# The Mamba state scan, cut into units of 32 channels times four states, with some of its B products on TensorE

## What is computed

```python
xdbl = jnp.einsum('ble,fe->blf', xc, xproj)           # xc: 512 channels, after conv and silu
dt = jax.nn.softplus(jnp.einsum('blr,er->ble', xdbl[..., :R], dtw) + dtb)
Bm, Cm = xdbl[..., R:R + NS], xdbl[..., R + NS:]      # NS = 16 states
def step(h, inp):
    dt_t, B_t, C_t, x_t = inp
    dA = jnp.exp(dt_t[..., None] * A)                 # A = -exp(Alog), one number per channel and state
    h = dA * h + (dt_t * x_t)[..., None] * B_t[:, None, :]
    y = jnp.einsum('ben,bn->be', h, C_t)
    return (h, y)
y = ssm_scan(dt, Bm, Cm, xc, A) + xc * Dp
y = y * jax.nn.silu(z)
```

## Times and profile before

| | |
|---|---|
| median of 3 runs | 3189.39 us (3189.24 to 3197.11) |
| the profiled execution | 3177.29 us |
| its span, first to last instruction | 3175.4 us |
| mean granted TensorE clock | 0.911 of full speed |
| layer 0 mixers, first to last scan | from 103.3 to 1051.3 us |
| layer 1 mixers | four chunks, to about 2808 us |

### The profile page before, as it was taken

How to read it: one execution, slowest core, us unless ns; L and a number is a source line. 1 busy time by engine, 2 the same in 40 slices (tenths; PEclk the granted TensorE clock), 3 DMA queues, 4 the chain that set the end, 5 groups by cost and what they waited for, 6 DMA issues and landing times. The chain is left out here.

```text
span 3175.4 us, 27412 instructions
## 1 busy us (share of the span) xinstructions
PE 2544.1 (80%) x8312; PEld 1195.9 (38%) x8312; DVE 1973.9 (62%) x2687; ACT 1386.0 (44%) x2120; POOL 1538.4 (48%) x1350
## 2 busy tenths in 40 slices
PE   5889989889978687678888459998488988768866
PEld 1333323333322254323333258886132332225422
DVE  1799999999999444666663400001349999953423
ACT  4566566566554333215555212221346555432243
POOL 2699999999998301300000320001449999940100
PEclk8999999999999889869999679998689999988887
DMA  1220220230220000253210434453222022000000
GB/s 65 108 107 24 106 108 22 92 114 8 99 107 0 20 1 0 89 66 41 41 21 2 148 119 173 173 192 114 65 107 84 24 106 106 2 20 0 0 8 27
DMA packets 69153, 215.25 MB, mean 68 GB/s; under 512 B 13692, under 2 KB 38536, under 8 KB 49944
## 3 DMA queue, kind: packets, MB, share of 16 engines
q1 hardware_dynamic: 62632, 181.11, 17.4%
q10 hardware_dynamic: 3312, 24.12, 2.3%
q0 software_dynamic: 3072, 8.39, 0.8%
HBM read 187.97 MB, written 25.43 MB: 67 GB/s over the span
## 5 line engine op out<-in xcount | busy, mean ns | idle before, releaser
L775 POOL TENSOR_TENSOR s_dbu<-s_dx,s_bc 128x512 f32<-128x512 f32 x768 | 964.6, 1281 | 47.2 <-DVE s_psum L509 43.4
L436 PE MATMUL s_psum<-s_hc,ident 128*128 128x512 f32 x1536 | 834.0, 633 | 174.1 <-DVE s_hc L529 163.0
L664 ACT ACTIVATE s_psum<-s_dt,s_a_neg 128x512 f32<-128x512 f32 x768 | 521.6, 688 | 586.1 <-DVE s_hc L529 585.1
L436 PEld LDWEIGHTS s_psum<-s_hc,ident 128*128 128x128 f32 x1536 | 260.3, 193 | 686.1 <-DVE s_hc L529 488.8
L529 DVE TENSOR_TENSOR s_hc<-s_psum,s_bc 128x512 f32<-128x512 f32 x624 | 421.8, 676 | 0.5 <-issue 0.5
L509 DVE TENSOR_TENSOR_SCAN s_psum<-s_psum,s_state,s_dbu 128x512 f32<-128x512 f32 x312 | 396.4, 1282 | 18.6 <-ACT s_psum L664 12.7
L509 DVE TENSOR_TENSOR_SCAN s_psum<-s_psum,s_dbu 128x512 f32<-128x512 f32 x312 | 381.4, 1223 | 22.1 <-ACT s_psum L664 14.2
L1467 ACT ACTIVATE s_probs<-s_banks 128x512 f32<-128x512 f32 (+3 forms) x384 | 169.7, 492 | 206.2 <-PE s_banks L1290 163.5
L163 POOL TENSOR_TENSOR s_pair<-s_res 128x512 f32<-128x512 f32 x8 | 10.0, 1267 | 416.0 <-issue 403.3
L1837 ACT ACTIVATE s_hidden<-s_banks,s_w 128x256 f32<-128x256 f32 x184 | 77.3, 471 | 302.3 <-PE s_banks L1660 302.3
L1858 POOL DMA_INDIRECT s_rows_in<-moe_out_rows,s_place x32 | 30.7, 958 | 358.4 <-DMA moe_out_rows<-s_ys 349.0
(11 more groups left out here) (260 smaller groups left out, 3638.1 us busy)
## 6 DMA issues: line engine op xcount, KB each, us to landing
s_bc<-fwd_rows SPq DMA_DIRECT2D x64, 1024.0 KB, 4.6
s_bc<-m_rows SPq DMA_DIRECT2D x32, 1024.0 KB, 4.7
s_w<-in_moe_w SPq DMA_DIRECT2D x23, 1028.0 KB, 7.2
s_w<-in_moe_w ACTq DMA_DIRECT2D x23, 1024.0 KB, 5.5
qk_parts<-s_parts SPq DMA_DIRECT2D x48, 128.0 KB, 1.9
s_stack_q<-qk_parts SPq DMA_DIRECT2D x48, 128.0 KB, 4.9
s_stack_k<-qk_parts SPq DMA_DIRECT2D x48, 128.0 KB, 8.2
moe_in_rows<-s_zero SPq DMA_DIRECT2D x1, 5888.0 KB, 18.9
```

Source lines behind the costliest of these rows:

```text
L436: pe.matmul(psum[:, SCANS + block_no % 2, :], consts["ident"][:], hc[:, unit % PRODUCTS, :], start=(n == 0), stop=(n == NS - 1)).then_inc( ...
L664: act.activation(psum[:, unit % SCANS, :], dt[:, g % 2, i // NS, :], ACT.Exp, scale=a_neg[CHUNKS[g][0]][:, i:i + 1]).then_inc(decay_ready, 1)
L775: pool.tensor_tensor(dbu[:, unit % TERMS, :], dx[:, g % 2, i // NS, :], bc[:, 2 * n, :], ALU.mult)\
```

## The change

A unit is now 32 channels times four states. Unit i has its block q = i // 16, a group n of four states and a strip j of 32 channels (`split`); partition r * 32 + e of its tile is state 4n + r of channel 32j + e.

- dt and dx have to stand four times, once for each r. Each block of both is stored to DRAM and read back by four DMAs of 32 partitions into `dt_rep` and `dx_rep` (two buffers each). B and C are spread by DMAs to 32 partitions; a tile of `b_rows` or `c_rows` then serves all strips and blocks.
- The sum over states: `total` multiplies with `fold` (four 32 x 32 identities on top of each other) and writes the 32 partitions of its strip. Four totals are now issued together, at every fourth unit.
- In 24 of 64 units (`TURNED`) the term dx * B is made by PE, in `turn_term`: 16 matmuls of transposed dx (stationary, 32 columns) with diagonal matrices of B (moving, 128 columns), into the unit's PSUM bank; ACT's decay goes to a `dbu` buffer there. PE does it three units ahead of the scan's, or four (`TURN_AT`). PE also transposes B and dx once a chunk (20 transposes), and ACT stores these and makes 32 diagonals of 128 x 128 (`make_diag`).
- `LENT` has 28 units in place of 12. Their scans write straight into `hc`, and POOL multiplies in place, `LAG` = 4 units later; in even chunks it first copies the last column to `state` and waits for that copy.
- `TERMS` is 4, `PRODUCTS` is 8. The remaining steps have new unit numbers; three of four gates are done within their own chunk.

The core of the diff (the second product, dx's store and spread and C's spread are written like their neighbours):

```diff
@@ -216,19 +216,51 @@
                 act.activation(rstd[:, c, :], rstd[:, c, :], ACT.Exp, scale=-0.5).then_inc(rstd_ready, 1)
 
 
+STRIP = 32
+STRIPS = P // STRIP
+GROUPS = NS // STRIPS
 UNITS = EB * NS
-SCANS, TERMS, PRODUCTS = 4, 3, 4
-LENT = [i < 3 * NS and i % 4 == 2 for i in range(UNITS)]
+SCANS, TERMS, PRODUCTS, LAG = 4, 4, 8, 4
+DIAG = (1, 3)
+LENT = [i in LENT_AT for LENT_AT in ((1, 3, 5, 7, 9, 11, 12, 13), (1, 2, 4, 5, 7, 9, 11, 12, 13), (5, 7, 12, 13),
+                                     (1, 3, 5, 7, 9, 12, 13)) for i in range(NS)]
+TURNED = [i % NS in (5, 7, 12, 13, 14, 15) for i in range(UNITS)]
+TURN_AT = {}
+for i in range(UNITS):
+    if TURNED[i]:
+        TURN_AT.setdefault(i - 4 if i % STRIPS == STRIPS - 1 else i - 3, []).append(i)
+MADE = [n for n in range(GROUPS) if not all(TURNED[n * STRIPS:(n + 1) * STRIPS])]
+KEEPS = sum(not (LENT[i] and LENT[i - 1]) for i in range(1, UNITS, 2))
...
+def split(i):
+
+    return i // NS, i // STRIPS % GROUPS, i % STRIPS
...
-        dt = s.sb("dt", [P, 2, EB, CH])
+        dt = s.sb("dt", [P, EB, CH])
-        bc = s.sb("bc", [P, 2 * NS, CH])
+        b_rows = s.sb("b_rows", [P, len(MADE), CH])
+        c_rows = s.sb("c_rows", [P, GROUPS, CH])
+        dt_rep = s.sb("dt_rep", [P, 2, STRIPS, CH])
+        dx_rep = s.sb("dx_rep", [P, 2, STRIPS, CH])
+        diag = s.sb("diag", [P, len(DIAG), STRIPS, CH // P, P])
+        b_cols = s.sb("b_cols", [P, CH // P, NS])
-        hs = s.sb("hs", [P, CH])
+        dt_d = core.nc.dram_tensor(f"{first}_steps", (2, EI, CH), F32, kind="Internal").ap()
+        dx_d = core.nc.dram_tensor(f"{first}_inputs", (2, EI, CH), F32, kind="Internal").ap()
...
-        for kind, count in (("x", EB), ("conv", EB), ("rows", 1), ("dt", EB)):
+        for kind, count in (("x", EB), ("conv", EB), ("rows", 1), ("dt", EB), ("cols", 1), ("turn", CH // P)):
...
-            def spread(g, n):
-                sp.dma_start(bc[:, 2 * n:2 * n + 4, :], rows_d[g % 2, 2 * n:2 * n + 4, :].partition_broadcast(P))\
-                  .then_inc(row_loaded[n // 2], 16)
+            def spread_b(g, n):
+
+                if g:
+                    sp.wait_ge(dbu_ready, made(g * UNITS - NS + (n + 1) * STRIPS))
+                for r in range(STRIPS):
+                    sp.dma_start(b_rows[r * STRIP:(r + 1) * STRIP, MADE.index(n), :],
+                                 rows_d[g % 2, 2 * (n * STRIPS + r), :].partition_broadcast(STRIP)).then_inc(b_loaded[MADE.index(n)], 16)
...
+            def store_dt(g, e):
+                sp.wait_ge(dt_ready, EB * g + e + 1)
+                sp.dma_start(dt_d[g % 2, e * P:(e + 1) * P, :], dt[:, e, :]).then_inc(dt_stored[e], 16)
+
...
+            def spread_dt(g, q):
+                block_no = EB * g + q
+                if block_no >= 2:
+                    sp.wait_ge(decay_ready, (block_no - 1) * NS)
+                sp.wait_ge(dt_stored[q], 16 * (g + 1))
+                for r in range(STRIPS):
+                    sp.dma_start(dt_rep[r * STRIP:(r + 1) * STRIP, q % 2, :, :],
+                                 dt_d[g % 2, q * P:(q + 1) * P, :].rearrange("(j e) t -> e j t", j=STRIPS))\
+                      .then_inc(dt_spread[q % 2], 16)
...
             store_rows(0)
-            for n in range(0, NS, 2):
-                spread(0, n)
+            for n in MADE:
+                spread_b(0, n)
+            for n in range(GROUPS - 1):
+                spread_c(0, n)
+            for q in range(2):
+                store_dt(0, q)
+                store_dx(0, q)
...
+            def turn_term(g, i):
+
+                unit = g * UNITS + i
+                q, n, j = split(i)
+                at = DIAG.index(n)
+                if unit >= SCANS and LENT[(unit - SCANS) % UNITS]:
+                    pe.wait_ge(scanned, unit - SCANS + 1)
+                elif unit >= SCANS:
+                    pe.wait_ge(product_ready, own(unit - SCANS + 1))
+                for w in (tile["turn", g, CH // P - 2], tile["turn", g, CH // P - 1]):
+                    pe.wait_ge(work_free[w % 2], w // 2 + 1)
+                pe.wait_ge(diag_ready, NS * (len(DIAG) * g + at + 1))
+                for b in range(CH // P):
+                    for r in range(STRIPS):
+                        mm = pe.matmul(psum[r * STRIP:(r + 1) * STRIP, unit % SCANS, b * P:(b + 1) * P],
+                                       turned_dx(g)[:, q, b, j * STRIP:(j + 1) * STRIP], diag[:, at, r, b, :],
+                                       start=True, stop=True)
+                mm.then_inc(term_turned, 1)
...
-                pe.matmul(psum[:, SCANS + block_no % 2, :], consts["ident"][:], hc[:, unit % PRODUCTS, :],
-                          start=(n == 0), stop=(n == NS - 1)).then_inc(product_used, 1)
+                pe.matmul(psum[j * STRIP:(j + 1) * STRIP, SCANS + block_no % 2, :], fold[:], hc[:, unit % PRODUCTS, :],
+                          start=(n == 0), stop=(n == GROUPS - 1)).then_inc(product_used, 1)
...
                 for i in range(UNITS):
-                    total(g, i)
-                    if g + 1 < NC and i < 16:
-                        conv(g + 1, i // TAPS, i % TAPS)
-                    if g and 16 <= i < 24:
-                        out(g - 1, (i - 16) // EB, i % EB)
-                    if g + 1 < NC and 24 <= i < 28:
-                        rows(g + 1, i - 24)
-                    if g + 1 < NC and i in (30, 31, 34, 35):
-                        steps_of(g + 1, (30, 31, 34, 35).index(i))
-                    if g and post is not None and 36 <= i < 38:
-                        var(g - 1, i - 36)
-                    if i in (38, 39) or 42 <= i < 48:
-                        in_z(g, (38, 42, 44, 46).index(i - i % KD), i % KD)
-                    if g + 2 < NC and 50 <= i < 58:
-                        in_x(g + 2, (i - 50) // KD, i % KD)
+                    for ahead in TURN_AT.get(i, ()):
+                        turn_term(g, ahead)
+                    if i % STRIPS == STRIPS - 1:
+                        for j in range(STRIPS):
+                            total(g, i - STRIPS + 1 + j)
+                    if g + 1 < NC and i < 8:
+                        conv(g + 1, i // 2, i % 2 * 2)
...
-                dve.wait_ge(dbu_ready, unit + 1)
-                h = psum[:, unit % SCANS, :]
-                if LENT[i] and lent(unit):
-                    dve.wait_ge(product_lent, lent(unit))
-                dve.tensor_tensor_scan(hs[:] if LENT[i] else h, h, dbu[:, unit % TERMS, :], begin, ALU.mult, ALU.add)\
-                   .then_inc(scanned, 1)
+                left, right = psum[:, unit % SCANS, :], dbu[:, unit % TERMS, :]
+                if TURNED[i]:
+                    dve.wait_ge(term_turned, turned(unit + 1))
+                    left, right = right, left
+                else:
+                    dve.wait_ge(dbu_ready, made(unit + 1))
+                if LENT[i] and unit >= PRODUCTS:
+                    dve.wait_ge(product_used, unit - PRODUCTS + 1)
+                h = hc[:, unit % PRODUCTS, :] if LENT[i] else psum[:, unit % SCANS, :]
+                dve.tensor_tensor_scan(h, left, right, begin, ALU.mult, ALU.add).then_inc(scanned, 1)
...
+                q, n, j = split(i)
+                to = psum[:, unit % SCANS, :]
                 if i % NS == 0:
-                    act.wait_ge(dt_ready, unit // NS + 1)
-                if unit >= SCANS and LENT[(unit - SCANS) % UNITS]:
+                    act.wait_ge(dt_spread[q % 2], 16 * STRIPS * (unit // NS // 2 + 1))
+                if TURNED[i]:
+                    to = dbu[:, unit % TERMS, :]
+                    if unit >= TERMS:
+                        act.wait_ge(scanned, unit - TERMS + 1)
+                elif unit >= SCANS and LENT[(unit - SCANS) % UNITS]:
                     act.wait_ge(scanned, unit - SCANS + 1)
                 elif unit >= SCANS:
                     act.wait_ge(product_ready, own(unit - SCANS + 1))
-                act.activation(psum[:, unit % SCANS, :], dt[:, g % 2, i // NS, :], ACT.Exp,
-                               scale=a_neg[CHUNKS[g][0]][:, i:i + 1]).then_inc(decay_ready, 1)
-
-            act.wait_ge(small_loaded, 32 * len(runs))
+                act.activation(to, dt_rep[:, q % 2, j, :], ACT.Exp, scale=a_neg[CHUNKS[g][0]][:, i:i + 1]).then_inc(decay_ready, 1)
...
+            def make_diag(g, at, k):
+
+                n, r, b = DIAG[at], k // (CH // P), k % (CH // P)
+                if g and k == 0:
+                    act.wait_ge(term_turned, turned(g * UNITS - NS + (n + 1) * STRIPS))
+                w = tile["cols", g, 0]
+                act.wait_ge(work_free[w % 2], w // 2 + 1)
+                act.activation(diag[:, at, r, b, :], consts["ident"][:], ACT.Copy,
+                               scale=b_cols[:, b, n * STRIPS + r:n * STRIPS + r + 1]).then_inc(diag_ready, 1)
...
-                    pool.wait_ge(dx_ready, unit // NS + 1)
+                q, n, j = split(i)
+                if i % NS == 0:
```

(35 more changed lines are left out.)

262 lines of the change are left out of this document (194 added, 68 removed).

## The result

| | before | after |
|---|---|---|
| median of the runs, us | 3189.3 (3185.4 to 3197.1, 4 runs) | 3318.3 (3315.5 to 3320.8, 4 runs) |
| profiled execution's span, us | 3175.4 | 3319.0 |
| mean granted TensorE clock, share of 2.4 GHz | 0.911 | 0.875 |
| ratio to before | 1 | 1.041 (1.038 to 1.043) |

The change makes the kernel 4.1% slower. The forecast was 3132 us and its range ended at 3210: wrong in sign and outside the range.

A forecast was written before the change was run, and what follows sets the result against it. DVE and POOL were taken to bound the kernel together. Twelve chunks at 5.6 us less gave -67, the two starts +10, so -57: profiled execution 3120, median 3132 us, range 3075 to 3210.

The forecast's parts named there:

- The start: Start of each call: stores and spreads of dt and dx delay the first scan from 103.3 to 108.3, 5 us.
- what is queued behind it: PE's waits at fours: the next turned terms, which DVE's scan needs, stand behind; covered by the extra microsecond of stalls.
- The bound: Mixer chunks: POOL's 109.3 us in even, DVE's 103.0 in odd, mean 106.2 against 112.8; with stalls 5.6 less a chunk.
- PE: 94 us of about 112, 84%: PE's work in a whole chunk: totals, turned units, other matmuls and transposes sum to 94 us, within the chunk's time.
- the 105: Sign of being wrong: PE above 105 us in a chunk.
- the microsecond of stalls: Each chunk: 1.0 us added to 4.5 of stalls, for more evenly loaded engines and PE's queue behind waits.
- Rival 3: Ahead of units 12 to 15 PE brings turned terms too late: 9.6 us a chunk longer, 3235 us; chance 0.08.
- If that is POOL's, it comes four units late: PE waits at each four of totals for the last product; counted within 1.0 us of extra stalls a chunk.
- I leave the clock as it is: TensorE clock in the mixers: taken as unchanged, 0.99 and 1.00 in the windows with PE at 90%.
- Rival 2: PE's fours of totals overlap only in part: 2.15 us each, 3206, chance 0.06; not at all: near 3450, chance 0.02.
- rival 4: ACT's longer stream eats the gain: new stalls of 5 us a chunk, 3189 within 10; chance 0.05.
- Rival 1: Deeper TERMS and PRODUCTS buffers also remove stalls, leaving 1.5 us a chunk: 9.6 less a chunk, 3084; chance 0.20.

The follow-up runs named there:

- e4_lent: Changed kernel with POOL's products moved off the last unit of each four (units 3, 7, 11 to 2, 6, 10): ratio 1.024 to the kernel before.
- e3_diag_once: Changed kernel making the 32 diagonals in the first chunk of each call only (output not the reference's): ratio 1.041 to the kernel before.
- e14_three: Changed kernel with all stores before spreads, POOL's products off each four's last unit, and three of four convolution matmuls omitted after a call's first chunk: 3184.2 us, ratio 0.998.
- e1_start: Changed kernel with the stores of all four blocks of dt and dx issued ahead of the first spread: ratio 1.029 to the kernel before.

## Why the prediction was wrong, point by point

The forecast put the profiled execution at 3120 us, and it took 3321. Of these 201 us, 46 are the two starts, 138 the twelve chunks and 17 the time outside the calls, for which the forecast had nothing.

- **The start, forecast +5 us a call, measured +28.** The failed step is "four spreads of dt and four of dx take 3.8 us to issue, so to 103.4, the last lands 3.5 us later". The issue was right (99.71 to 103.36), and the first spread landed 3.3 us after its issue, near the 3.5 taken. But the eight landed 1.2 us apart and not 0.47, so the last came at 111.3 in place of 106.9; this path would have cost 9 us by itself (111.4 + 1.2 - 103.3). The trace before had shown this: the eight spreads of the earlier trace rows, 1 MB each and issued in 3.8 us, landed 2.5 us apart, the first after 4.5 us and the eighth after 18.6, of which the median in the earlier trace rows tells nothing. The other 19 us are a path that had no term: ACT's copy of the turned dx, a new instruction ahead of the first decay, waits for all four blocks, and SP issues the stores of two of them behind block 1's spreads. The prediction had asked of a wait "what is queued behind it" only for PE.
- **The bound, forecast 5.6 us a chunk less; measured 8.1 more in ten chunks, 5.3 less in two.** The loads of DVE and POOL were right. The failed step is "PE: 94 us of about 112, 84%", a chunk's sum held against a chunk's time. PE's in-order stream had 30.8 us of work for the first quarter, in which DVE takes 26. The sum was low besides: PE is busy 102.0 us in chunk 1, where little of the clock is lost, and 107 to 109 in four of layer 0's eight chunks, over the 105 that the prediction named as a sign of being wrong.
- **The last chunks' 5.3 us are no success of the forecast.** They are odd chunks, and for an odd one its loads say 112.3 to 103.0, 9.3 less, or 8.3 with the microsecond of stalls. DVE's busy time did fall so (112.4 to 104.0 and 110.3 to 100.8), but its idle time rose from 2.5 and 2.0 us to 5.5 and 6.2. That this comes near the mean of 5.6 is chance.
- **Rival 3** named the place (units 12 to 15) and the in-order queue. Its "up to three other matmuls between them" is right for the terms among themselves; what it left out is ahead of them, eleven matmuls of 512 columns between the four of units 0 to 3 and unit 12's term. Its price was 2.4 us at each of four places, 9.6 a chunk; measured are 62.4 us in eight chunks, 7.8 each, but unevenly: 5.2 to 5.9 us in the first quarter, 0 to 3.3 in the others. Its 3235 fell short because it kept the forecast's start, stalls and clock, and its chance of 0.08 was far too low. The sentence that DVE's idle time on PE would be over 20 us in layer 0 if it held proved the right mark: 62 us.
- **"If that is POOL's, it comes four units late"** was written down as part of 1.0 us of stalls a chunk. It measured 52 us in twelve chunks (e4_lent), 4.3 each, a part of it through the clock: the term of the sum that was mis-sized most in the chunks.
- **"I leave the clock as it is"** failed. The mean granted clock of the ten chunks' second quarters is 0.86, in the kernel before 1.00, and a quarter that falls costs about 5 us. The earlier trace rows could not show this, for they are taken with a PE that had a total to do at every unit.
- **Rival 2, refuted.** Eight records of four totals, each total with its own wait and increment, take 524.11 - 523.13 = 0.98 us. Taken singly, the four totals' first records start from 523.135 to 523.155, and only then their second ones, which carry the increments, from 523.564 to 523.584; one record after the other takes 0.43. The Trainium skill, "TensorE: Matmul & The Clock Gate", Part 3, has matmuls start and end in strict program order. This trace does not agree for the records of float32 matmuls: a total's second record stands ahead of the next total's first in the program (where a four's last product was late, two totals' second records started at 511.74 and the fourth's first at 514.70), and here it starts behind it.
- **Terms that held:** a turned term 1.01 us (forecast 1.0 to 1.4; taken 1.2); POOL's multiply 0.26 us after the copy's start (0.27); the scans' pitch with exchanged operands, 1.13 us in even chunks (1.13) and 1.17 to 1.19 in odd ones (1.19); ACT's work in a chunk about 81 us (83), its diagonals 0.30 us each, and no cost from them (e3_diag_once), so rival 4's cause did not act.
- **Rival 1** (deeper buffers take the stalls away) can be seen in no chunk: even in the last ones DVE's idle time is longer than before.

## What to carry to other kernels

Hold an engine's load against the time of the stretch in which it is placed, not against the whole loop: 94 of 112 us hid 30.8 of 26. An in-order engine that is given work in groups waits for the latest member of the group, and everything behind it waits too, so let the group's last input come from the fastest producer. At a loop's start follow every engine's stream up to its first instruction that the loop needs, not only the data's path, and price a burst of DMAs by how far apart they land, not by a median.

## What the runs showed of the hardware

- Four column groups of 32 columns overlap even when every matmul has its own wait and increment: 0.97 to 1.00 us for four of 512 columns in float32 (0.98 above), and 1.86 us at the lower clock level (e14_three, chunk 5).
- The same instructions of one program ran a quarter at a granted clock of 1.00 or 0.76, in two chunks of one execution and in the same chunk of two, 29.6 or 34.9 us. Adding 1.8 us of matmuls in the gap ahead did not stop the fall in even chunks; eight matmuls more in the last chunks' first quarter did (0.72 to 1.00). What the chip goes by stays open.
- DMAs issued 0.47 us apart on one queue landed 1.2 us apart when each wrote 256 KB of spread dt or dx, and 2.5 us apart when each spread 1 MB of B and C (the kernel before). The last 1 MB of eight spreads of 256 KB had landed 10.4 us after its first issue (e1_start).
- Left open: the third quarter's 1.3 us more than before, the 3 us by which e14_three's chunks miss the forecast, and the 17 us outside the calls, of which only the last output matmuls' wait (1.7 us) and the lower clock were seen, not tested.
